# A fused attention and mixture-of-experts layer: expert stages ahead of the attention heads, and half of the combination beside the heads

## The chip, the cores and the metric

The kernel runs on one core of a Trainium2 chip. The metric is the device time of one execution in microseconds. The engines are TensorE (PE, with its weight loads PEld), VectorE (DVE), ScalarE (ACT), GpSimd (POOL) and SyncE (SP, which here only issues DMAs). Each engine works through its own instruction list in order, and waits on semaphores for the others.

## What is computed

Input x is 8 batches of 512 tokens of 256 numbers, that is 32 token tiles of 128 tokens. All is float32. In short:

```python
xn = layernorm(x)
# attention: 16 heads, low-rank queries (128) and keys/values (64), rotary part of 64, causal softmax
attn_out = attention(xn) @ W_o
# experts: 32 experts of width 96, 6 chosen for each token, and a shared one of width 192
scores = sigmoid(xn @ gate_w); w, i = top_k(scores, 6); w = w / sum(w)
routed = sum over the 6 chosen e of w[e] * (silu(xn @ wg[e]) * (xn @ wu[e])) @ wd[e]
shared = (silu(xn @ sg) * (xn @ su)) @ sd
out = x + attn_out + routed + shared
```

## The kernel before

A float32 product is made of three matmuls of rounded parts (`product3`, lines 58 to 63: high by high, low by high, high by low), so each operand is split into a high and a low part by ACT and DVE. The kernel is a row of blocks; a block begins when every engine has ended the one before.

1. Weights, then `project` (line 228): for each of 8 batches the layer norm, the latents and the routing. SP stores the results to memory and fills the first half of `sorted_x` with zeros, 2 MB for each batch (line 335). At its end DVE works out which expert owns which tile and in which row of `sorted_x` each token goes (`routes`, from line 588). I call this stage tokens.
2. `heads` (line 641): 8 batches, 16 heads each. A step of the pipeline is one head, two steps are a pair. `pipeline` runs the first 8 steps alone, then a loop from the middle of one batch to the middle of the next. PE's step is scores, queries or their transposes, scores, values, scores, transposes of the probabilities, scores; DVE takes the maxima (line 1066), turns queries by rope (lines 1047 to 1052), copies and divides. Beside this POOL scatters all 32 token tiles into `sorted_x`, 6 indirect DMAs each (line 816), and SP fills the second half of `sorted_x` with zeros in the first batches (line 773). The residual sum goes to `res_dram`.
3. `weights_and_shared` (line 1381): 16 steps. Each loads and splits the weights of two experts and computes the shared expert of one token tile.
4. `sorted_tiles` (line 1502): 256 tiles of 128 rows sorted by expert, in two groups of 128, each group from 16 token tiles. While the second group is computed, `Combine` adds up the six expert rows of 15 token tiles of the first group: POOL gathers them (line 1333), DVE finds the six shares (line 1353) and adds (line 1374).
5. `shared_and_rest` (line 1738): the shared expert of the last 16 token tiles, and the combination of the last 17.

The lines that set a token tile's combination are:

```python
for k in ks:
    ins = dve.scalar_tensor_tensor(self.found[:, k, :], self.slot_of[:, m, :], self.slot_top[:, m, k:k + 1],
                                   self.comb[:, m, :], ALU.is_equal, ALU.mult, accum_out=self.share[:, k:k + 1])
...
dve.wait_ge(self.s["summed"], TOPK * m + TOPK + k)
dve.scalar_tensor_tensor(self.sum[par][:], self.rows[par][u][:, place, :], self.share[:, k:k + 1],
                         last[:], ALU.mult, ALU.add).then_inc(self.s["summed"], 1)
```

## Time and profile before

| | us |
|---|---|
| median of 3 runs (1851.81 to 1855.62) | 1854.5 |
| the profiled execution, its own time | 1855.27 |
| its span, first to last instruction | 1853.5 |
| PE busy | 1467.5 (79%) |
| DVE busy | 1115.1 (60%) |
| ACT busy | 930.9 (50%) |
| POOL busy | 569.7 (31%) |

The granted clock of PE over the whole is 0.895 of full speed. The shares of the whole span hide what differs from stage to stage, so the work below is read stage by stage: which engine is busy there, at which clock, and how busy the DMA engines are.

### The profile page before, as it was taken

The page shows a single profiled execution, that of the slowest core. Times are in us where ns is not written, and L with a number is a line of the kernel's source. Part 1 is how long each engine was busy: PE and PEld are TensorE (multiplying, and loading weights), DVE is VectorE, ACT ScalarE, POOL GpSimd, SP SyncE. Part 2 cuts the span into 40 slices and gives each one's busy share as a digit, 9 for nine tenths or more (in the row PEclk, how much of TensorE's full clock was granted, in tenths as well). Part 3 has the DMA queues.
Part 4 walks back from the last instruction along what each step waited for, and adds up shares of the span by engine and source line. Part 5 has one row for each costly group of instructions (what it writes and reads, how often), then busy time and mean ns, then how long its engine had stood idle before and what let it go on. Part 6 is the DMA issues. An engine that isn't in the chain of part 4 may idle for free. (4 is left out here: it accounts for less than half of the span.)

```text
span 1853.5 us, 37109 instructions
## 1 busy us (share of the span) xinstructions
PE 1467.5 (79%) x10112; PEld 1248.0 (67%) x10113; DVE 1115.1 (60%) x4335; ACT 930.9 (50%) x2739; POOL 569.7 (31%) x640
## 2 busy tenths in 40 slices
PE   2663499989899999999999986799998888885340
PEld 2552378868688777878878764588887777774330
DVE  2896276656566676766666644555555666664464
ACT  1330276656566666666666644366665555552000
POOL 1120043433343343433433430000001433335565
PEclk8676699999999999999999997799999998998665
DMA  3993611321411111111111107654545665665553
GB/s 143 329 375 123 232 56 56 113 88 47 147 58 60 49 52 60 58 62 58 58 54 47 50 21 239 201 163 157 159 153 163 197 184 183 193 194 179 148 168 112
DMA packets 169539, 240.29 MB, mean 130 GB/s; under 512 B 16786, under 2 KB 142738, under 8 KB 165010
## 3 DMA queue, kind: packets, MB, share of 16 engines
q1 hardware_dynamic: 146322, 183.61, 29.9%
q0 software_dynamic: 18432, 50.36, 8.8%
q10 hardware_dynamic: 4608, 4.20, 0.8%
q8 instruction: 82, 1.34, 0.3%
q14 instruction: 95, 0.78, 0.1%
HBM read 115.42 MB, written 122.68 MB: 128 GB/s over the span
## 5 line engine op out<-in xcount | busy, mean ns | idle before, releaser
L988 ACT ACTIVATE prob<-prob,negmax 128x512 f32<-128x512 f32 (+3 forms) x512 | 285.3, 559 | 302.1 <-DVE negmax L1066 300.8
L1066 DVE CUSTOM_DVE_ANT_0 prob<-ps,mask_add 128x512 f32<-128x512 f32 (+3 forms) x512 | 244.2, 485 | 147.4 <-issue 144.2
L61 PE MATMUL ps<-kt_hi,qt_hi 128*128 (+4 forms) x512 | 188.5, 368 | 21.7 <-issue 18.7
L816 POOL DMA_INDIRECT sorted_x<-xn_row,row_no x192 | 188.3, 981 | 49.4 <-issue 45.0
L826 POOL TENSOR_TENSOR spread<-rinv,one 128x512 f32<-128x512 f32 x64 | 66.6, 1040 | 380.0 <-DVE rinv L1072 380.0
L63 PE MATMUL ps<-kt_hi,qt_lo 128*128 (+4 forms) x512 | 166.4, 325 | 0.0
L62 PE MATMUL ps<-kt_lo,qt_hi 128*128 (+4 forms) x512 | 166.0, 324 | 0.0
L910 PE MATMUL ps<-ident,prob 128*128 128x128 f32 x1280 | 160.6, 273 | 0.0
L926 PE MATMUL ps<-pt,nkv 128*64 128x512 f32 (+3 forms) x1024 | 152.0, 439 | 2.3 <-DVE lat L1084 2.3
L910 PEld LDWEIGHTS ps<-ident,prob 128*128 128x128 f32 x1280 | 143.5, 140 | 0.2 <-ACT prob L988 0.2
L1001 ACT ACTIVATE pt<-ps 128x1024 f32<-128x1024 f32 (+2 forms) x130 | 130.4, 1003 | 19.8 <-PE ps L910 16.9
L1680 ACT ACTIVATE hidden<-ps 128x96 f32<-128x96 f32 x256 | 64.5, 252 | 124.7 <-PE ps L63 108.3
L926 PEld LDWEIGHTS ps<-pt,nkv 128*64 128x64 f32 x1024 | 68.2, 136 | 86.5 <-issue 74.6
L1692 ACT ACTIVATE rows_out<-ps 128x256 f32<-128x256 f32 x256 | 98.5, 385 | 49.7 <-PE ps L63 34.7
L1076 DVE COPY pt<-ps 128x512 f32<-128x512 f32 x128 | 88.0, 687 | 57.1 <-PE ps L910 57.1
L61 PEld LDWEIGHTS ps<-kt_hi,qt_hi 128*128 128x128 f32 x512 | 98.2, 192 | 35.1 <-issue 30.2
L821 POOL TENSOR_TENSOR lat_lo<-lat,lat_hi 128x512 fp32r<-128x512 f32 x64 | 81.7, 1277 | 109.6 <-ACT lat_hi L1006 109.6
L1720 DVE TENSOR_TENSOR act_f<-hidden,ps 128x96 f32<-128x96 f32 x256 | 64.8, 253 | 80.8 <-ACT hidden L1680 61.9
L1331 POOL TENSOR_TENSOR carrier_b<-one_b 128x1 f32 x30 | 5.9, 196 | 343.9 <-DMA sorted_y<-rows_out 223.4
L61 PE MATMUL ps<-wq_hi,nqt 128*128 128x256 f32 x256 | 74.5, 291 | 45.2 <-DMA nqt<-nqt_dram 45.2
L1635 PE MATMUL ps<-ident,rows_in 128*128 128x128 f32 x512 | 103.6, 285 | 6.2 <-DMA rows_in<-sorted_x 5.9
L1333 POOL DMA_INDIRECT rows_c<-sorted_y,idx_c x102 | 99.6, 976 | 27.5 <-issue 26.5
(240 smaller groups left out, 4481.4 us busy)
## 6 DMA issues: line engine op xcount, KB each, us to landing
sorted_x<-zeros SPq DMA_DIRECT2D x16, 2048.0 KB, 9.4
rows_in<-sorted_x SPq DMA_DIRECT2D x128, 256.0 KB, 2.8
sorted_y<-rows_out SPq DMA_DIRECT2D x128, 256.0 KB
nqt<-nqt_dram SPq DMA_DIRECT2D x16, 512.0 KB
raw_gu<-in_wgu SPq DMA_DIRECT2D x16, 384.0 KB, 4.0
x_in<-in_x SPq DMA_DIRECT2D x8, 512.0 KB, 4.2
xn_dram<-xn SPq DMA_DIRECT2D x8, 512.0 KB, 5.0
xnt_dram<-xnt_hi SPq DMA_DIRECT2D x16, 256.0 KB, 4.7
```

Source lines behind the costliest of these rows:

```text
L61: pe.matmul(out, lh, rh, start=first, stop=False, **kw)
L62: pe.matmul(out, lh, rl, start=False, stop=False, **kw)
L63: return pe.matmul(out, ll, rh, start=False, stop=last, **kw)
L816: pool.indirect_dma_start(sorted_x, bass.IndirectOffsetOnAxis(ap=row_no[par][:, k:k + 1], axis=0), xn_row[par][:], None).then_inc(scattere ...
L910: mm = pe.transpose(pt_ps[:, at:at + P], prob[:, g % 2, qt, kt * P:(kt + 1) * P], ident[:])
L926: mm = pe.matmul(o_ps[par * KVR:(par + 1) * KVR, kt * P:S], nkv[half][:, kt, :], pt[:, par, PT_AT[kt]:PT_AT[kt] + w], start=kt == 0, stop= ...
L988: act.activation(prob[:, i, qt, 0:w], prob[:, i, qt, 0:w], ACT.Exp, bias=negmax[:, i, qt:qt + 1], scale=-1.0, accum_out=rowsum[:, g // 2 % ...
L1001: act.activation(pt[:, g % 2, lo:hi], pt_ps[:, lo:hi], ACT.Copy).then_inc(pt_act, 1)
L1066: dve.tensor_tensor_reduce(prob[:, i, qt, 0:w], s_ps[k % 2][:, 0:w], mask[:, S - w:S], -1.0, -MASKED, ALU.add, ALU.min, negmax[:, i, qt:qt ...
L1333: pool.indirect_dma_start(self.rows[par][u][:, k, :], None, self.sorted_y, bass.IndirectOffsetOnAxis(ap=self.idx[par][u][:, k:k + 1], axis ...
L1635: mm = pe.transpose(xt_ps[par][:, kc * P:(kc + 1) * P], rows_in[j // 2 % AHEAD][:, par, kc * P:(kc + 1) * P], ident[:])
L1692: act.activation(rows_out[d % 2][:, (j - 3) % 2, :], y_ps[1 - par], ACT.Copy)\
```

## The change

The stages change places. After tokens comes `weights_and_shared`, now with all 32 token tiles and the weights of one expert a step, while POOL scatters the 16 token tiles of the first group. Then `sorted_tiles`: beside its first half POOL writes zeros where rows are unused (16 indirect DMAs in place of the plain fill of the second half) and scatters the second group; beside its second half the 15 token tiles are combined as before, into `base_dram`. `heads` comes last, adds its residual to `base_dram` and writes `out`; beside its first batches 17 token tiles are gathered and added. `shared_and_rest` is gone. As the heads now run later, keys, query weights and output weights are stored to memory in tokens and loaded again. Cut to its core:

```diff
@@ build
-            attention(nc, ctx, sem, x, wc, ...)
-        experts(nc, sem, wgu, wd, ...)
+            tokens(nc, ctx, sem, x, wc, ...)
+        experts(nc, sem, x, wgu, wd, ...)
+        with ExitStack() as ctx:
+            heads(nc, ctx, sem, rope, nqt_dram, kt_dram, nkv_dram, wq_dram, wvo_dram, base_dram, sorted_y, ...)
@@ project, SP
                 sp.dma_start(nqt_dram[i], nqt[:].bitcast(F32)).then_inc(nq_stored, 16)
+                sp.dma_start(kt_dram[i], kt[:].bitcast(F32)).then_inc(kt_stored, 16)
             load(0)
+            for k in range(2):
+                sp.dma_start(wq_dram[k], wq_s[k][:].bitcast(F32)).then_inc(kept, 16)
+                sp.dma_start(wvo_dram[k], wvo_s[k][:].bitcast(F32)).then_inc(kept, 16)
@@ routes: nine DVE instructions for the rows to be filled with zeros, behind the tiles' owners
+                chain(dve.tensor_copy(pad_no[:], pad_f[:]))
@@ heads, the token tile of a step: four steps (phases) for one token tile
+        def token_tile(self, g):
+            if not self.gathers or g >= NH:
+                return None
+            if g < NH // 2 and self.last is None:
+                return (0, 0, 0, g) if g < QUART else None
+            i, at = (self.now, g - NH // 2) if g >= NH // 2 else (self.last, g + NH // 2)
+            j, phase = divmod(at, QUART)
+            return QUART * i + (j + 1), (j + 1) % 2, 2 * i + (j + 1) // 2, phase
@@ heads, pipeline
+            batches(0, QUART, True)
+            if after_gathers is not None:
+                after_gathers()
+            batches(QUART, B - 1, False)
@@ heads, SP
-            def fill(i):
-                sp.dma_start(zero_part[i], zeros[:]...)
+                sp.wait_ge(s_ready, TT * NH * b + TT * NH // 2)
+                sp.dma_start(kt[0][:].bitcast(F32), kt_dram[b + 1]).then_inc(kt_loaded[0], 16)
@@ heads, POOL, in a step after the spreading and the low parts
-                if g < NH and par == 1:
-                    scatter(bt.now, g // 4, g // 2 % 2)
+                if bt.token_tile(g):
+                    c, buf, _, phase = bt.token_tile(g)
+                    if phase == 0:
+                        gather(c, buf)
@@ heads, DVE, in a step after the residual and ahead of the maxima
-                    dve.tensor_copy(row_no[q % 2][:], slot_no[:, TT * bt.now + q, :]).then_inc(row_no_ready, 1)
+                    if phase == 0:
+                        copy_indices(c, buf, n)
+                    if phase < 2:
+                        find_shares(c, buf, HALFK * phase)
+                    else:
+                        for k in range(HALFK * (phase - 2), HALFK * (phase - 1)):
+                            add_row(c, buf, n, k)
@@ weights_and_shared
-    EC = NE // GT
+    EC = NE // NT
+            def load_row(t):
+                if t >= 2:
+                    sp.wait_ge(scattered[t % 2], 16 * TOPK * (t // 2))
+                sp.dma_start(xn_row[t % 2][:], xn_dram[t]).then_inc(row_loaded[t % 2], 16)
+        @block.gpsimd
+        def _(pool):
+            for t in range(GT):
+                pool.wait_ge(row_loaded[t % 2], 16 * (t // 2) + 16)
+                for k in range(TOPK):
+                    pool.indirect_dma_start(sorted_x, bass.IndirectOffsetOnAxis(ap=slot_no[:, t, k:k + 1], axis=0),
+                                            xn_row[t % 2][:], None).then_inc(scattered[t % 2], 16)
@@ sorted_tiles, SP (load_row as above, once in 4 pairs) and POOL
+                    if ms[-1] is None and d % EVERY == 0:
+                        load_row(i, d // EVERY)
+            for k in range(2 * PADS):
+                pool.indirect_dma_start(chunks, bass.IndirectOffsetOnAxis(ap=pad_no[:, k:k + 1], axis=0),
+                                        zeros[:], None).then_inc(padded, 16)
@@ the last stage
-def shared_and_rest(nc, ctx, shared, combine):
-    ...
```

## Rows read from the trace of the kernel before

**Rows 1.** Busy time by stage; columns: stretch, engines busy (x), PEclk, DMA share, GB/s

```profile
0.00:202.60 202.60, 89.00 (x448) 74.26 (x449) 119.06 (x512) 43.61 (x172) 25.04 (x29) 0.71 0.61 222
202.60:1117.30 914.70, 839.81 (x6144) 703.11 (x6144) 584.99 (x2241) 560.38 (x1410) 341.60 (x353) 0.98 0.21 73
1117.30:1194.60 77.30, 55.44 (x224) 41.09 (x224) 42.78 (x100) 33.27 (x83) 0.00 (x0) 0.76 0.79 240
1194.60:1418.00 223.40, 208.45 (x1577) 187.73 (x1577) 118.82 (x401) 144.86 (x524) 0.10 (x1) 0.96 0.50 158
1418.00:1679.40 261.40, 215.58 (x1496) 191.88 (x1496) 159.85 (x674) 135.63 (x500) 94.33 (x120) 0.92 0.60 184
1679.40:1853.50 174.10, 59.24 (x224) 49.93 (x224) 89.58 (x408) 13.15 (x50) 108.61 (x137) 0.62 0.52 155
```

**Rows 2.** POOL's end of the heads block (L763) and of the last (L1767)

```profile
L763 POOLq DRAIN  x1: 8034/8034/8034, 1102.4 to 1102.4; - x1
L1767 POOLq DRAIN  x1: 18298/18298/18298, 1835.0 to 1835.0; - x1
```

**Rows 3.** Tokens: one batch's busy time, and SP's wait at the stage's end

```profile
112.20:125.10 12.90, 8.94 (x40) 7.71 (x40) 11.87 (x57) 4.22 (x21) 2.65 (x2) 0.66 1.05 376
SPq L313 <- DMA tile_expert<-owner: 36.1, 1, 36.1
```

**Rows 4.** Weights and shared: four steps' busy time; what ACT waits for, 1130 to 1190

```profile
1145.00:1160.00 15.00, 12.26 (x48) 9.31 (x48) 9.44 (x22) 7.45 (x20) 0.00 (x0) 0.77 0.91 279
ACT wgu_hi L1475 <- DMA raw_d<-in_wd: 29.7, 14, 3.0
```

**Rows 5.** Indirect DMAs on POOL: two lines (duration ns min/median/max), one in the timeline

```profile
L1333 POOL DMA_INDIRECT rows_c<-sorted_y,idx_c x102: 940/949/1263, 1680.5 to 1843.8; - x102
L816 POOL DMA_INDIRECT sorted_x<-xn_row,row_no x192: 957/963/1501, 223.9 to 1087.9; - x192
1703.36 0.94 POOL L1333 DMA_INDIRECT rows_c<-sorted_y,idx_c  x1 [0.31 <-issue]
```

**Rows 6.** Sorted tiles: PE's transposes in 1215:1400 and 1440:1670, and POOL's DMA queue in 1440:1670

```profile
L1635 PE MATMUL ps<-ident,rows_in 128*128 128x128 f32 x222 | 43.2, 276 | 0.0
L1635 PE MATMUL ps<-ident,rows_in 128*128 128x128 f32 x223 | 46.0, 289 | 0.0
q0 software_dynamic: 4032, 11.02, 17.2%
```

**Rows 7.** Last stage, DVE's groups of the combination

```profile
L1374 DVE SCALAR_TENSOR_TENSOR sum_c<-rows_c,share_c,sum_c 128x256 f32<-128x256 f32 x85 | 41.6, 489 | 8.2 <-DMA rows_c<-sorted_y,idx_c 5.6 <-DVE sum_c L1374 0.5
L1353 DVE SCALAR_TENSOR_TENSOR found_c<-slot_of,slot_top,comb 128x32 f32 (+1 forms) x102 | 18.9, 244 | 0.1
```

**Rows 8.** Heads, one pair of steps in the timeline: DVE twice, then PE

```profile
702.20 0.55 DVE L1066 CUSTOM_DVE_ANT_0 prob<-ps,mask_add 128x384 f32<-128x384 f32 x1 [1.25 <-issue]
705.96 0.69 DVE L1084 TENSOR_TENSOR lat<-ps,pt 128x512 f32<-128x512 f32 x1
706.89 2.37 PE L926 MATMUL ps<-pt,nkv 128*64 128x512 f32 x16
```

**Rows 9.** Heads: a pair without residual; and the last gather's issue with its first reader

```profile
661.44 1.04 POOL L826 TENSOR_TENSOR spread<-rinv,one 128x512 f32<-128x512 f32 x1 [4.17 <-DVE rinv L1072]
670.25 0.29 DVE L1066 CUSTOM_DVE_ANT_0 prob<-ps,mask_add 128x128 f32<-128x128 f32 x1
...
1843.83 1.08 POOL L1333 DMA_INDIRECT rows_c<-sorted_y,idx_c  x1 [0.30 <-issue]
1846.70 1.52 DVE L1374 SCALAR_TENSOR_TENSOR sum_c<-rows_c,share_c,sum_c 128x256 f32<-128x256 f32 x3 [2.10 <-DMA rows_c<-sorted_y,idx_c]
```

**Rows 10.** Heads: PE's idle time at three loop starts, in the timeline

```profile
377.64 0.79 PE L61 MATMUL ps<-kt_hi,qt_hi 128*128 x1 [6.32 <-issue]
493.29 0.79 PE L61 MATMUL ps<-kt_hi,qt_hi 128*128 x1 [6.28 <-issue]
824.08 0.49 PE L61 MATMUL ps<-kt_hi,qt_hi 128*128 x1 [2.17 <-issue]
```

More of the change, by code:

```diff
@@ L1181, with __init__ @@
+            sorted_tiles(nc, part, sem, combine, wgu_s, wd_s, sorted_x, sorted_y, tile_expert, xn_dram,
+                         slot_no, pad_no, ident, ps)
 class Shared:
-    def __init__(self, nc, ctx, tag, times, sems, sgu, sd, xnt_dram, res_dram, base_dram, ident, ps):
+    def __init__(self, nc, ctx, sem, sgu, sd, x, xnt_dram, base_dram, ident, ps):
         def two(name, shape, dt=F32):
-            return [ctx.enter_context(nc.sbuf_tensor(f"{name}{i}_{tag}", shape, dt)) for i in range(2)]
+            return [ctx.enter_context(nc.sbuf_tensor(f"{name}{i}", shape, dt)) for i in range(2)]
@@ L1398, in steps @@
             step(n, n % 2, n // 2)
-        with eng.Fori(2, GT // 2) as i:
+        with eng.Fori(2, NT // 2) as i:
             for par in range(2):
                 step(2 * i + par, par, i)
-        for n in range(GT, GT + 2):
+        for n in range(NT, NT + 2):
             step(n, n % 2, n // 2)
     def tile(n, lag):
-        return not isinstance(n, int) or 0 <= n - lag < GT
+        return not isinstance(n, int) or 0 <= n - lag < NT
     def parts(n, par, half):
@@ L1579, in body @@
                     r = PAIRS * i + d
+                    if ms[-1] is None and d % EVERY == 0:
+                        load_row(i, d // EVERY)
+                    if ms[-1] is None and not isinstance(i, int) and d == PAIRS - AHEAD + 1:
+                        for par in range(2):
+                            sp.wait_ge(scattered[par], 16 * TOPK * ((ROWS // 2 + 1) * i - 1))
                     if not (isinstance(i, int) and r + AHEAD - 1 >= NTILE // 2):
```

506 lines of the change are left out of this document (269 added, 237 removed).

## Prediction, made before the result was known

> **What bounds the kernel now.** I read busy time by stage first [rows 1]. The six stages take 202.6, 914.7, 77.3, 223.4 and 261.4 (the two halves of the sorted tiles) and 174.1 us, together 1853.5. PE fills 92% of heads and 93% of the first half of the sorted tiles, at a clock of 0.98 and 0.96: there PE sets the pace. The last stage is different: PE is busy for 59.2 of 174.1 us at a clock of 0.62, DVE for 89.6, POOL for 108.6. It waits for POOL's gathers, and no other work lies beside them. The change takes this stage away and lays its work beside others. So the question is what its two parts, 16 shared tiles and 17 combined tiles, cost in their new places, and what the reordering adds in memory traffic.
>
> **The last stage goes: minus 174.1 us.** All of it lies on the path, as blocks follow one another. Its end includes POOL's drain, which ran until 1853.3, some 5 us past the last sum [rows 2]. The new end is the end of heads, where POOL's drain (8.0 us from 1102.4) was over before PE's last matmuls, so only the store of the residual and the block's end follow, and these are inside the 914.7 already.
>
> **Tokens: plus 12 us.** Added are eight stores of keys (0.5 MB each), 4 MB of weights at the start, and nine small DVE instructions. The nine (2 to 3 us) lie behind the owners' step; SP waits 36.1 us for the two tiny `tile_expert` stores issued before them [rows 3], and DVE was idle in that wait, so they cost nothing, and 3 us if that wait were gone. A batch takes 12.9 us, with DVE busy 11.87 and the DMA engines' share at 1.05, 376 GB/s [rows 3]: both are full. 0.5 MB more at 376 GB/s is 1.4 us a batch, 11 us for eight, if DMA binds; if the queue had room it would be some 0.5 us, 4 us in all. The 4 MB at the start would take 11 us at that rate, but fall where the first batch has hardly any traffic; 1 to 11 us. I take 9 + 3 = 12, ends 3 and 22.
>
> **Weights and shared: plus 70 us.** There are 32 steps in place of 16. Four steps took 15 us, 3.75 each, at a DMA share of 0.91 and 279 GB/s, and ACT waited 29.7 us for weights [rows 4]. A step moved 1.09 MB: weights 0.58, tokens 0.25, residual and sum 0.25. A new step moves half the weights (0.29), the same 0.5, and of the scatter 0.38 and its rows 0.06: 1.23 MB. At 279 GB/s and full use (279/0.91 = 307) that is 4.0 us. POOL needs six indirect DMAs for two steps, each 0.95 with a gap of 0.31 [rows 5]: 7.6 us, 3.8 a step, so it is nearly as late. PE's 12.26 us for four steps [rows 4] are 3.1 a step and don't bind. I take 4.05 us a step: 130, and the 77.3 - 60 = 17 us of filling and emptying stay, 147 in all. The SP queue now has a wait for the scatter of two tiles ago ahead of each row load, with the loads of tokens and weights queued behind it; it is satisfied while POOL keeps to 7.6 us. Ends: 3.75 (plus 60 us) and 4.8 a step (plus 93).
>
> **Sorted tiles: plus 10 us.** The second half keeps its work. Beside the first half POOL now issues 112 indirect DMAs: 112 x 1.26 = 141 us, inside 223.4. They carry 21 MB, at the q0 price of 17.2% of 230 us for 11.02 MB [rows 6], 3.6 us a MB, 76 us of the DMA engines: the share goes from 0.50 to some 0.85. No engine of that half waited for loads, so this hides. What doesn't is SP: the third row load waits until POOL has done 16 zero DMAs and the first token tile (22 x 1.26 = 28 us, and landing), and SP's loads and stores for PE and ACT stand behind it; again at the end, when SP waits for the last scatter. Each block is 8 to 11 us with some 5 to 9 us of loads ahead: 5 us each. Ends 0 and 35 (if the larger share slows each tile as the second half's traffic may have).
>
> **Heads: plus 34 us.** Three terms. (a) The zero fills go. PE stood for 6.3 us at the first two loop starts, while 4 MB of fill were under way, and 2.2 at a later one [rows 10]: minus 2 x 4.2 = 8.5. (b) At the start PE waits for half a MB of query weights more: plus 1; the rest (keys, 3.5 MB) lands while the first steps run. (c) DVE gets, in four steps for each of 17 token tiles: phase 0 a copy (as before) and three shares, 3 x 0.244 = 0.7 us; phase 1 0.7; phases 2 and 3 three additions, 3 x 0.489 = 1.5 each [rows 7]. They stand ahead of the maxima and, in odd steps, of the division `lat`. In an even step DVE had 1.25 us idle behind the first maxima [rows 8]: phase 0 hides, phase 2 shows 0.25. In an odd step DVE ends `lat` at 706.65 and PE begins its values, which need that bank, at 706.89: slack 0.24, so phase 1 shows 0.46 and phase 3 1.26. Sum 1.95, times 17 is 33 us. PE has no other slack to give it back. Then the gathers. POOL's six follow the spreading, at 662.5 [rows 9]: some 0.2 for the carrier, 6 x 1.26 to issue; the last begins at 669.0, and a reader can start 2.87 us after its issue begins (1843.83 to 1846.70) [rows 9]: 671.9. DVE comes for them at 670.5 in pairs without a residual, so it waits 1.4 us, of which some 1 shows, for 8 of 17 tiles: 8 us. In pairs with one it comes 2 us later and doesn't wait. Heads: -8.5 + 1 + 33 + 8 = 34. Ends: nothing of (c) shows (minus 8), and all of it does, 17 x 4.4 + 16 = 91 (plus 83). For comparison, the same additions beside the sorted tiles: 223 transposes, 112 tiles, in 230 us against 112 in 185 [rows 6] is 45 us for 14 token tiles, 3.2 us each of some 4.7; heads' 1.95 is less because I can name the idle time.
>
> **The sum.** 1853.5 - 174.1 + 12 + 70 + 10 + 34 = 1805.4 us of span. The profiled execution took 1855.27 for a span of 1853.5, 1.8 more, so 1807.2 against 1855.27, and the median shown is 0.8 below that: 1806 us, 2.6% faster.
>
> **The rivals.** *A, as above*: 0.61. *B, PE hides DVE's new work*: DVE goes from 64% of heads to some 80% in the first batches, still short of full; then (c) is nothing: 1806 - 42 = 1764 us. Against it speaks the slack of 0.24 us; 0.14. *C, memory traffic binds the early stages*: the shared steps take 4.8 us (+23), the sorted tiles lose 25 more, tokens 10 more: 1806 + 48 or less, say 1840. For it speaks a share of 0.91 before anything is added, against it the half-size weights; 0.15. *D, the gathered rows come late*: DVE waits for them with the maxima, and so PE, queued behind it. 42 us of lead plus what I count already make this decide from 48/17 = 2.8 us of further lateness per token tile. A gather that took 1.9 us on POOL instead of 0.95 would be 5.7 us later, 17 x 5.7 = 97: 1903 us. Against it: a scatter beside the heads took 0.963 us, a gather in the last stage 0.949 [rows 5], so the busy DVE does not slow POOL; 0.10.
>
> The Trainium skill has a rule that speaks for D and against this change. "SBUF — State Buffer", sections "SBUF: two separate sides" and "Who interferes with whom", says in substance that POOL can't write the descriptors of its DMAs while DVE runs an instruction that takes the ports both share, and gives 620 ns against 3100 ns for such a DMA. By that factor of five, six gathers would be late by far more than D's 2.8 us and the kernel slower than before. The trace doesn't show it: 963 against 949 ns.
>
> **How the numbers follow.** The likeliest is A, 1806. B reaches down to 1764, C up to 1840, my bounds of the single terms some 15 to 20 us each way for those that go together. I leave out the ends of B and C and all of D: 1758 to 1848, and the range reaches lower than higher about 1806 because B is a whole case and its lower bounds (tokens 9 less, weights 10 less) go with it. A difference of 0.2%, 3.7 us, is about what a measurement of this kernel can tell from none. Faster: A and B, and most of C: 0.87. Same: 0.02. Slower: D and the tail of C: 0.11.
>
> **What would show it.** Tokens end near 215 us. The weights stage takes 147 with a DMA share of 0.9 or more, and POOL nearly without gaps. The first half of the sorted tiles has two gaps of some 5 us on PE, at its start and end, and no others. In heads the first four loop batches take some 8 us longer each than the last three, PE waits before its values (L926 of before) for DVE's division, and the 6.3 us stalls are 2.2. It would be wrong if PE's waits in heads were behind gathered rows (D), if all batches took the same time (B), or if PE in the sorted tiles waited for loads (C).

## The result, and the profile after

The changed kernel took 1944.8 us (median of 4 runs, 1943.2 to 1953.0) beside 1853.2 for the kernel before (median of 4, 1850.8 to 1855.6): a ratio of 1.050, 95% interval 1.047 to 1.054. It is 5% slower, where I forecast 2.6% faster. Its profiled execution took 1943.6 us for a span of 1941.8.

The same kind of table as [rows 1], for the kernel after: a stretch, then its length, the busy time of PE, PEld, DVE, ACT and POOL with the number of instructions, the granted clock of PE, the share of the DMA engines and GB/s. The five stretches are tokens, weights and shared tiles, the two halves of the sorted tiles, and heads.

```profile
0.00:211.80 211.80, 87.36 (x448) 73.07 (x449) 123.82 (x527) 42.74 (x172) 25.42 (x30) 0.71 0.68 252
211.80:388.50 176.70, 112.94 (x448) 90.02 (x448) 64.86 (x196) 48.87 (x163) 93.84 (x96) 0.67 0.71 235
388.50:721.60 333.10, 252.33 (x1579) 229.19 (x1580) 119.96 (x401) 149.20 (x525) 108.61 (x114) 0.79 0.54 175
721.60:980.40 258.80, 217.77 (x1496) 195.08 (x1494) 158.75 (x673) 136.44 (x500) 92.63 (x120) 0.90 0.61 186
980.40:1941.80 961.40, 848.27 (x6144) 708.32 (x6144) 647.59 (x2534) 562.96 (x1411) 249.51 (x250) 0.98 0.17 53
```

Against [rows 1], stage by stage, with what I had forecast in brackets: tokens +9.2 (+12), weights and shared +99.4 (+70), first half of the sorted tiles +109.7 (+10), second half -2.6 (0), heads +46.7 (+34), last stage -174.1 (-174.1). The sum is +88.3, against -48. Of the 136 us between them, 100 lie in one term, the first half of the sorted tiles, and 29 in the shared stage. Neither stage ran out of anything that I had counted: the DMA share is 0.54 and 0.71, not 0.85 and 0.9, and POOL's scatters keep their pace (961 ns, as in [rows 5]), while POOL itself mostly waits for the next token tile's rows, which SP loads once in four pairs of sorted tiles:

```profile
L1780 POOL DMA_INDIRECT sorted_x<-xn_row_e,slot_no x96 | 92.3, 961 | 201.1 <-DMA xn_row_e<-xn_dram 169.3
```

**One burst of scatters.** Eight sorted tiles took 19.2 us, against 13.2 in the kernel before ([rows 6]: 112 tiles in 185 us). In the 7.6 us in which POOL issues the six scatters of a token tile PE does 36 matmuls and transposes; in the 11.6 us behind it, 66, at a clock of 0.75:

```profile
483.40:491.00 7.60, 4.72 (x36) 3.97 (x35) 1.83 (x7) 2.37 (x8) 5.76 (x6) 0.94 0.60 183
491.00:502.60 11.60, 10.35 (x66) 9.52 (x66) 5.38 (x19) 6.52 (x24) 0.00 (x0) 0.75 0.47 143
```

From the timeline of that burst (lines between these are left out): start, duration, engine, line, operation, names, and in brackets the idle time before it and what ended it.

```profile
488.05 0.28 PE L67 MATMUL ps<-wgu_hi,xt_e0lo 128*128 x1
488.49 0.96 POOL L1780 DMA_INDIRECT sorted_x<-xn_row_e,slot_no  x1 [0.30 <-issue]
489.17 0.25 ACT L1863 ACTIVATE hidden<-ps 128x96 f32<-128x96 f32 x1 [2.55 <-PE ps L67]
489.45 0.26 DVE L1903 TENSOR_TENSOR act_f<-hidden,ps 128x96 f32<-128x96 f32 x1 [2.37 <-ACT hidden L1863]
489.76 0.31 PE L1836 MATMUL ps<-ident,act_f 128*96 128x128 f32 x1 [1.44 <-issue]
```

The reader is to see the first and third lines. The last matmul of the gate and up product ends at 488.33, ACT has long been idle, and yet it begins the activation that waits for that product at 489.17, 0.84 us later. No load is waited for. A sorted tile passes through ten handings-over between PE, ACT and DVE, and four of them go out from PE. In these rows only that kind is late: DVE begins 0.03 us after ACT has ended (489.42 to 489.45), PE 0.05 us after DVE (489.71 to 489.76). In the whole half, wherever DVE stood waiting for ACT's part of a tile, it began within 0.04 us of ACT's end, while ACT came up to 1.4 us late behind PE's transposes. PE's ends are modelled in this profile, so these rows don't tell whether PE's signal is late or its result.

**Heads.** The engine waits of PE in heads (engine, line, what it waited for: us in total, times, longest) are mostly where I had put them: the values (L1020, L926 of before) wait for DVE's division, the waits that end in "issue", those at loop starts among them, are at most 2.2 us in place of the 6.3 of [rows 10], and the first wait is for query weights. The longest in total (L961) is no news, the kernel before has it too (33.0 us). But the scores wait 22.2 us for DVE's maxima (`negmax`), 2.3 in the kernel before, and there I had allowed 0.25 us a token tile.

```profile
PE ps L961 <- DVE qp L1157: 35.0, 62, 3.0
PE ps L1020 <- DVE lat L1220: 25.7, 27, 2.0
PE ps L65 <- DVE negmax L1202: 22.2, 22, 2.2
PE ps L65 <- DMA wq_lo_h<-wq_dram: 12.1, 1, 12.1
PE ps L65 <- issue: 7.3, 10, 2.2
```

The stores of the residual, one a batch, show the two kinds of batches: 124.3 and 123.6 us apart with gathered tiles beside them, 110.4 without. I had said some 8 us between them; it is 14.

```profile
1153.16 0.41 SPq L880 DMA_DIRECT2D out<-res  x1
1277.45 0.41 SPq L880 DMA_DIRECT2D out<-res  x1
...
1633.84 0.41 SPq L880 DMA_DIRECT2D out<-res  x1
1744.28 0.41 SPq L880 DMA_DIRECT2D out<-res  x1
```

### The profile page after: what moved, and what is told of

Same layout as the page of the kernel before. It is cut to its first block and busy times, and to the rows that moved or that the text cites. A ratio compares the mean times of both kernels' runs of the same rounds, so it can differ in the third digit from the quotient of the medians.

```text
span 1941.8 us, 37055 instructions
## 1 busy us (share of the span) xinstructions
PE 1518.7 (78%) x10112; PEld 1295.7 (67%) x10113; DVE 1115.0 (57%) x4331; ACT 940.2 (48%) x2770; POOL 570.0 (29%) x610
## 3 DMA queue, kind: packets, MB, share of 16 engines
q0 software_dynamic: 20736, 58.75, 9.4%
## 5 line engine op out<-in xcount | busy, mean ns | idle before, releaser
L1202 DVE CUSTOM_DVE_ANT_0 prob<-ps,mask_add 128x512 f32<-128x512 f32 (+3 forms) x512 | 244.1, 487 | 150.2 <-issue 145.8
L65 PE MATMUL ps<-kt,qt_hi 128*128 128x512 f32 (+3 forms) x512 | 190.7, 372 | 29.1 <-DVE negmax L1202 22.2
L1020 PE MATMUL ps<-pt,nkv 128*64 128x512 f32 (+3 forms) x1024 | 152.0, 438 | 28.2 <-DVE lat L1220 25.7
L66 PE MATMUL ps<-kt,qt_hi 128*128 128x512 f32 (+3 forms) x512 | 166.2, 325 | 0.0
L67 PE MATMUL ps<-kt,qt_lo 128*128 128x512 f32 (+3 forms) x512 | 165.6, 323 | 0.0
L1780 POOL DMA_INDIRECT sorted_x<-xn_row_e,slot_no x96 | 92.3, 961 | 201.1 <-DMA xn_row_e<-xn_dram 169.3
L1020 PEld LDWEIGHTS ps<-pt,nkv 128*64 128x64 f32 x1024 | 74.7, 136 | 108.0 <-issue 89.8
L1004 PEld LDWEIGHTS ps<-ident,prob 128*128 128x128 f32 x1280 | 144.5, 141 | 0.2 <-ACT prob L1093 0.2
L1106 ACT ACTIVATE pt<-ps 128x1024 f32<-128x1024 f32 (+2 forms) x130 | 130.2, 1002 | 16.1 <-PE ps L1004 13.2
L1594 POOL DMA_INDIRECT sorted_x<-xn_row,slot_no x96 | 93.8, 978 | 127.3 <-DMA xn_row<-xn_dram 99.2
L65 PEld LDWEIGHTS ps<-kt,qt_hi 128*128 128x128 f32 x512 | 97.7, 191 | 49.0 <-DVE negmax L1202 29.3
L65 PE MATMUL ps<-wgu_hi,xt_e1hi 128*128 x256 | 89.6, 350 | 48.5 <-DVE xt_e1lo L1897 36.1
L1818 PE MATMUL ps<-ident,rows_in 128*128 128x128 f32 x512 | 113.0, 307 | 7.3 <-DMA rows_in<-sorted_x 5.8
L1836 PE MATMUL ps<-ident,act_f 128*96 128x128 f32 x256 | 80.5, 314 | 47.1 <-issue 26.4
```

The source lines that it names most:

```text
L65: pe.matmul(out, lh, rh, start=first, stop=False, **kw)
L66: pe.matmul(out, lh, rl, start=False, stop=False, **kw)
L67: return pe.matmul(out, ll, rh, start=False, stop=last, **kw)
L1004: mm = pe.transpose(pt_ps[:, at:at + P], prob[:, g % 2, qt, kt * P:(kt + 1) * P], ident[:])
L1020: mm = pe.matmul(o_ps[par * KVR:(par + 1) * KVR, kt * P:S], nkv[half][:, kt, :], pt[:, par, PT_AT[kt]:PT_AT[kt] + w], start=kt == 0, stop= ...
L1106: act.activation(pt[:, g % 2, lo:hi], pt_ps[:, lo:hi], ACT.Copy).then_inc(pt_act, 1)
```

## The experiments

The theories at the start: **H**, while POOL issues indirect DMAs and they are under way, every handing-over between the other engines takes longer, whatever the bytes (the rows above show it too wide: only those out of PE); **B**, the added bytes; **S**, the row loads and waits on SP's queue. As blocks follow one another, a stage can be read alone, and one kernel can carry a different alteration in each. Runs were spread over several chips, and that turned out to matter as much as any alteration, so I give for each run the time of the kernel before beside it.

**Without indirect DMAs.** The six scatters or gathers of a token tile are gone, and the pads; a small POOL instruction raises the semaphore.

```diff
-                for k in range(TOPK):
-                    pool.indirect_dma_start(sorted_x, bass.IndirectOffsetOnAxis(ap=slot_no[:, GT + t, k:k + 1], axis=0),
-                                            xn_row[t % 2][:], None).then_inc(scattered[t % 2], 16)
+                pool.memset(idle_second[:, t:t + 1], 0.0).then_inc(scattered[t % 2], 16 * TOPK)
```

> The changed kernel without any indirect DMA: the scatters of both groups, the pads, and the gathers of the second half of the sorted tiles and of heads are left out, and the semaphores are raised by small POOL instructions instead. Left out of the computation: what these rows would carry (DVE adds rows of zeros, with the same instructions). The row loads on SP's queue stay, with their waits. The second half of sorted_x is filled with zeros at the end of the tokens stage (16 MB), which makes that stage some 30 to 50 us longer, so only the stages behind it are read. Theory H (while POOL issues indirect DMAs and they are under way, every handing over between PE, ACT and DVE takes about 1 us longer, whatever the bytes; PE's clock falls after the stalls): the first half of the sorted tiles falls from 333 to 223-230 us with a clock of 0.95, the shared stage from 177 to 125-135 us. Theory B (the added bytes): the same here. Theory S (the waits and row loads on SP's queue): both stay near 333 and 177. Second half of the sorted tiles (259): 223-230 if the gathers cost its 35 us over the first half of before, 255-260 if DVE's additions do, as I wrote. Heads (961): 950 if gathers only cost the 8 us of lateness of my forecast; 915-930 if H holds there too.

Measured, beside 1786.3 of the kernel before: shared 114.2, first half 224.8, second half 210.7, heads 941.1. On this chip S falls: the row loads and their waits are all there. The second half was a surprise: some 50 us less than in either kernel's own profile (258.8 and 261.4), with all of DVE's additions in it.

**Narrow rows.**

```diff
+NARROW = 16
...
-                    pool.indirect_dma_start(sorted_x, bass.IndirectOffsetOnAxis(ap=slot_no[:, GT + t, k:k + 1], axis=0),
-                                            xn_row[t % 2][:], None).then_inc(scattered[t % 2], 16)
+                    pool.indirect_dma_start(narrow, bass.IndirectOffsetOnAxis(ap=slot_no[:, GT + t, k:k + 1], axis=0),
+                                            xn_row[t % 2][:, 0:NARROW], None).then_inc(scattered[t % 2], 16)
```

> The changed kernel with every indirect DMA kept, same count, same indices, but 64 bytes of a row instead of 1024 (scatters into and gathers from a tensor of its own; the pads stay as they are). Left out of the computation: the other 960 bytes of each row (the additions run over zeros there). Sorted_x is filled with zeros at the end of tokens, as in the kernel without indirect DMAs. H: what counts is that POOL issues them, so the first half of the sorted tiles stays at 320-335 us and the shared stage at 170-177. B: the bytes are a sixteenth, so the first half falls to 225-235 and the shared stage to 130. The second half and heads go the same way: unchanged (259, 961) by H, as without indirect DMAs by B.

**Direct DMAs on POOL's queue.**

```diff
-                    pool.indirect_dma_start(sorted_x, bass.IndirectOffsetOnAxis(ap=slot_no[:, GT + t, k:k + 1], axis=0),
-                                            xn_row[t % 2][:], None).then_inc(scattered[t % 2], 16)
+                    pool.dma_start(sorted_x[(GSORT + TOPK * t + k) * P:(GSORT + TOPK * t + k + 1) * P],
+                                   xn_row[t % 2][:]).then_inc(scattered[t % 2], 16)
```

> The changed kernel with every scatter and gather turned into a direct DMA of the same bytes on POOL's queue (fixed rows; the pads stay indirect). Left out: the rows go to and come from wrong places. H in its narrow form (only indirect DMAs, whose descriptors POOL writes itself, do it): first half of the sorted tiles 225-240 us, shared 125-140. B: same bytes, so 320-335 and 170-177. If direct DMAs on POOL's queue are written by POOL as well and cost about as much per DMA as the indirect ones, H too gives 320-335, and the narrow kernel decides alone.

**Additions over one column.**

```diff
-                dve.scalar_tensor_tensor(total[par][:], rows[par][:, k, :], share[par][:, k:k + 1],
-                                         (base if k == 0 else total)[par][:], ALU.mult, ALU.add)
+                dve.scalar_tensor_tensor(total[par][:, 0:1], rows[par][:, k, 0:1], share[par][:, k:k + 1],
+                                         (base if k == 0 else total)[par][:, 0:1], ALU.mult, ALU.add)
```

> The changed kernel with all DMAs, but the six additions of a token tile run over 1 column instead of 256, in the second half of the sorted tiles and in heads (left out of the computation: the other 255 columns of the combination). The first half and the shared stage stay at 333 and 177 by every theory. My forecast took the second half's 35 us over the first half of before as the additions' price: then it falls from 259 to 223-230. If the gathers cost it (H), it stays at 250-259. Heads: my forecast has 1.95 us of additions and shares visible per token tile, most of it additions: 961 falls to 930-935; if H rules there, it stays at 950-961.

The four ran one after the other on one chip. Shared, first half, second half, heads: narrow 141.0, 239.0, 210.4, 948.5; direct 131.2, 239.5, 210.9, 943.9; additions over one column 143.5, 243.5, 211.6, 931.3. The last kernel's first two stages are the changed kernel's, word for word, and took 143.5 and 243.5, not 176.7 and 333.1. Nothing that I had altered could do that.

```profile
215.10:358.60 143.50, 92.09 (x448) 77.94 (x448) 64.00 (x196) 48.04 (x163) 95.85 (x96) 0.82 0.87 290
358.60:602.10 243.50, 215.36 (x1579) 195.58 (x1580) 119.35 (x401) 144.58 (x525) 108.44 (x115) 0.92 0.73 240
```

**Both kernels again.** So I ran the two kernels unaltered, and the changed one with one part undone: no scatters of the second group (the first diff above) and no pads.

```diff
-            for k in range(2 * PADS):
-                pool.indirect_dma_start(chunks, bass.IndirectOffsetOnAxis(ap=pad_no[:, k:k + 1], axis=0),
-                                        zeros[:], None).then_inc(padded, 16)
+            pool.memset(idle_pads[:], 0.0).then_inc(padded, 32 * PADS)
```

> The changed kernel unaltered, in the company of the kernel before, because the stages that four altered kernels share with it word for word ran shorter there than in its own profile (the shared stage 143.5 us where only the sums were cut, against 176.7), and the kernel before took 1786 us beside them, not 1853. Theory P (the length of the early stages depends on something outside the kernel, the chip or where its tensors lie): 1770 to 1800 us, ratio 0.99 to 1.01, with a shared stage of 144 and a first half of the sorted tiles of 220-240. Theory F (the ratio of 1.05 belongs to the kernel): 1875 where before takes 1786, with the first half at 333 us again.

> The kernel before unaltered, for a profile under the same conditions as the altered kernels. If it takes 1786 us again: P says that the 67 us under 1853 lie in the stages with POOL's indirect DMAs beside short handings-over, the second half of the sorted tiles (261 down to 225-235) and the last stage (174 down to 140-150), while tokens, heads and the first half, which has no indirect DMA, keep 203, 915 and 223. If the difference lay in PE's clock or in heads, heads would be 50 us shorter.

> The changed kernel without the second group's scatters and pads (left out: these rows; the second half of sorted_x is filled with zeros at the end of the tokens stage, which makes that stage 30 to 50 us longer). Only the first half of the sorted tiles has something taken away. H (handings-over are slower while indirect DMAs run): that half goes to 223-230, wherever it stands with them; the shared stage is as in the changed kernel beside it (177 or 144), the second half 259 or what it is there.

On this chip the changed kernel is the faster one, by 0.6%: 1771.6 us (4 runs, 1769.0 to 1772.3) against 1781.6 (7 runs, 1779.1 to 1785.1), ratio 0.994, 95% interval 0.992 to 0.996. Theory P holds, F falls. The stages of the kernel before there, in the order of [rows 1]:

```profile
0.00:205.90 205.90, 86.25 (x448) 72.48 (x449) 119.12 (x512) 43.55 (x172) 25.01 (x29) 0.72 0.60 218
205.90:1119.90 914.00, 838.51 (x6144) 701.21 (x6144) 585.07 (x2241) 560.51 (x1410) 341.50 (x353) 0.98 0.21 73
1119.90:1196.50 76.60, 52.93 (x224) 38.62 (x224) 42.80 (x100) 33.27 (x83) 0.00 (x0) 0.81 0.78 242
1196.50:1419.20 222.70, 208.12 (x1577) 187.63 (x1577) 118.85 (x401) 144.99 (x524) 0.10 (x1) 0.96 0.50 158
1419.20:1633.30 214.10, 197.15 (x1497) 175.88 (x1496) 161.87 (x674) 136.67 (x500) 92.20 (x120) 0.98 0.74 225
1633.30:1782.80 149.50, 58.00 (x224) 49.37 (x224) 88.74 (x408) 13.01 (x50) 108.48 (x137) 0.63 0.60 180
```

Against [rows 1] two stages differ by more than 4 us: the second half (214.1 for 261.4) and the last stage (149.5 for 174.1). They are the two in which POOL's indirect DMAs run beside short handings-over; heads, with 192 scatters, doesn't differ (914.0 for 914.7). And the changed kernel's stages there:

```profile
0.00:215.60 215.60, 87.74 (x448) 72.91 (x449) 123.82 (x527) 42.60 (x172) 25.42 (x30) 0.69 0.67 247
215.60:360.10 144.50, 92.54 (x448) 78.82 (x448) 64.58 (x196) 48.45 (x163) 95.83 (x96) 0.82 0.88 288
360.10:603.60 243.50, 214.62 (x1579) 194.57 (x1580) 119.62 (x401) 144.97 (x525) 108.69 (x114) 0.92 0.74 240
603.60:817.90 214.30, 195.91 (x1496) 174.73 (x1494) 161.04 (x673) 135.57 (x500) 92.33 (x120) 0.99 0.73 224
817.90:1770.50 952.60, 844.72 (x6144) 706.70 (x6144) 650.13 (x2534) 563.29 (x1411) 250.14 (x250) 0.98 0.17 53
```

A burst of six scatters and the time up to the next one, in the same kernel on this chip: PE does 59 matmuls in the 7.6 us, not 36, its clock stays at 1.00, and the eight tiles take 13.4 us, not 19.2. The activation that waited 0.84 us above follows its product (ends 457.89) within 0.04 us.

```profile
429.10:436.70 7.60, 7.25 (x59) 6.70 (x59) 3.80 (x13) 5.03 (x18) 5.78 (x6) 1.00 0.74 228
436.70:442.50 5.80, 5.58 (x45) 4.96 (x45) 3.57 (x12) 3.79 (x16) 0.00 (x0) 1.00 0.65 204
```

```profile
457.62 0.27 PE L67 MATMUL ps<-wgu_hi,xt_e1lo 128*128 x1
457.93 0.25 ACT L1863 ACTIVATE hidden<-ps 128x96 f32<-128x96 f32 x1 [0.40 <-PE ps L67]
```

With the second group's scatters and pads undone the first half took 224.2, the other stages 143.4, 214.2 and 953.4, as they were.

The end of the shared stage there (in the changed kernel on this chip; duration in ns min/median/max, then first and last start) shows what sets its length. The last matmul begins at 347.99, but POOL issues its last scatter at 349.4, its drain at the block's end then takes 7.9 us, and only behind that does the next stage begin, at 360.1:

```profile
L1594 POOL DMA_INDIRECT sorted_x<-xn_row,slot_no x96: 958/963/1341, 223.1 to 349.4; - x96
L1552 POOLq DRAIN  x1: 7902/7902/7902, 352.0 to 352.0; - x1
```

Here POOL itself is the last to end: 96 scatters at 1.26 us are 121 of the 144.5 us, and 8 more are the drain. On the slow chip PE's work and POOL's drain end within 1.5 us of each other.

From here on I speak of two kinds of chips. On **kind 1** the kernel before takes 1777 to 1786 us (three chips), on **kind 2** 1851 to 1864 (four chips more, and the runs of the case itself). None lay between. Each chip was met in one session only, so "kind of chip" is a name: a difference of session or of where the tensors lie would look the same. What makes the kind no run shows.

**The causes on kind 2.** Which kind a run meets can't be chosen, so the next kernels ask one question a stage, with the edits shown above in other combinations.

> The changed kernel with a different alteration in each stage, as blocks follow one another and each stage is read alone. Shared stage: no scatters. First half of the sorted tiles: no pads, the 96 scatters kept but with 64 bytes a row instead of 1024 (into a tensor of its own). Second half: no gathers, additions kept. Heads: no gathers, additions kept. All these rows are left out of the computation; sorted_x and the narrow tensor are filled with zeros at the end of tokens, which lengthens that stage by 30 to 50 us. Two answers by the time of the kernel before beside it. Where that is 1780 to 1786: shared 114, first half 235-240 (count, not bytes, costs 10-15 us), second half 211, heads 940. Where it is 1850 to 1855, H (on such a chip each handing-over takes longer while indirect DMAs are under way, whatever the bytes): shared 114-120, first half 300-333 with 64 bytes as with 1024, second half down from 259 to 211-220, heads down from 961 to 940-950. If bytes are the cause there: first half 225-240, the second half down as well. If such a chip is slow by itself, without any indirect DMA: shared stays above 140 and the second half at 259.

It met kind 2 (1858.2 beside it):

```profile
245.80:359.60 113.80, 84.85 (x448) 71.99 (x448) 63.53 (x196) 47.57 (x163) 1.57 (x16) 0.89 0.84 255
359.60:683.90 324.30, 247.17 (x1589) 225.21 (x1590) 120.15 (x403) 148.33 (x527) 94.72 (x102) 0.82 0.39 118
683.90:890.50 206.60, 192.66 (x1486) 171.71 (x1484) 162.05 (x672) 136.66 (x497) 5.70 (x30) 1.00 0.56 175
890.50:1833.30 942.80, 843.63 (x6144) 705.61 (x6144) 649.49 (x2534) 563.21 (x1411) 154.41 (x150) 0.99 0.12 40
```

Without scatters the shared stage is as on kind 1 (113.8 and 114.2), so the chip is not slow by itself, and S falls here too, as the row loads and their waits are in it. With 64 bytes a row, and no pads, the first half still takes 324.3, at a DMA share of 0.39: bytes are not the cause, B falls. Without gathers, with all additions, the second half drops from 258.8 to 206.6.

> The changed kernel, altered by stages. Shared stage: the 96 scatters kept, with 64 bytes a row. First half of the sorted tiles: no pads; the scatters turned into direct DMAs of the same bytes on POOL's queue (fixed rows). Second half: gathers with 64 bytes a row, additions kept. Heads: gathers kept, additions over one column in place of 256. Rows and sums left out accordingly; the zero fill at the end of tokens as in mix_a. Where the kernel before takes 1780-1786 beside it: 141, 235-240, 211 and 931 us. Where it takes 1850-1858, H (each DMA that POOL issues while others pass work to and fro costs about 1 us, bytes don't count) has shared 165-177, the second half 250-259 with 64 bytes as with 1024. For the first half it leaves two answers that this run tells apart: 300-325 if every DMA written by POOL does it, 225-250 if only indirect ones do. Heads there: 961 less the additions' visible part, 930 by my forecast's sizes.

> The changed kernel, altered by stages. Shared stage as it is. First half of the sorted tiles: the six scatters of a token tile no longer in one burst of 7.6 us but one for every 1.33 tiles that PE turns (for the first twelve token tiles). Second half: gathers kept, additions over one column (left out: the rest of these sums). Heads: the six gathers of a token tile in two threes, one step apart, as the kernel before scattered its rows. Where the kernel before takes 1780-1786: 144, 235-243, 212 and 945-953 us. Where it takes 1850-1858: if the loss is a price of each DMA (H), the first half stays at 315-335 however they lie; if it comes from bursts, in which descriptors pile up, it falls to 240-280. Second half: 250-259, since additions cost nothing there (mix_a lost 52 us of 259 by leaving out the gathers alone). Heads: 961 by a price of each DMA, 945 by bursts.

Both met kind 1 (1777.1 beside them). The direct and narrow forms: shared 140.6 (narrow), first half 236.4 (direct, no pads), second half 206.4 (narrow), heads with additions over one column 927.5. The other kernel's edit is a wait ahead of each scatter and, in heads, two threes in place of six gathers:

```diff
+                    if t < 12:
+                        pool.wait_ge(xt_ready, 8 * t + 2 + 4 * k // 3)
...
-                    if phase == 0:
-                        gather(c, buf)
+                    if phase < 2:
+                        gather(c, buf, phase)
```

It gave 143.4, 244.1 (spreading does nothing on kind 1), 211.7, and heads of 995.9, 43 us more than with six gathers in one go, where I had expected none: the last three rows now come a step later, and DVE waits for them ahead of its maxima. Of DVE's waits in the first batches of heads (813.9 to 1400 us), those for gathered rows; the changed kernel on kind 1 has 3.7 us in 4 such waits, none longer than 1.2:

```profile
DVE total L1187 <- DMA rows<-sorted_y,idx: 31.3, 12, 4.5
```

This is the mechanism of rival D.

> The changed kernel, altered by stages. Shared stage: direct DMAs on POOL's queue in place of the scatters, same bytes, fixed rows. First half of the sorted tiles: pads and scatters kept, each scatter gated on the tiles PE has turned, so that they lie 1.33 tiles apart. Second half: direct DMAs in place of the gathers, additions kept. Heads: gathers kept, additions over one column. Rows and sums are wrong or left out accordingly. Where the kernel before takes 1780-1786: 131, 244, 211 and 928-931 us, as in the altered kernels before. Where it takes 1850-1858, against 177, 333, 259 and 961 of the changed kernel: if every DMA that POOL writes does it, shared 155-177 and the second half 245-259; if only indirect ones do, 115-135 and 206-220. First half 315-335 if each scatter has its price, 240-290 if the bursts do it. Heads 930-940.

It met kind 2 (1857.5 beside it):

```profile
216.00:347.90 131.90, 91.61 (x448) 78.01 (x448) 64.48 (x196) 48.22 (x163) 51.59 (x96) 0.82 0.94 315
347.90:637.30 289.40, 234.27 (x1579) 209.83 (x1580) 118.75 (x401) 143.59 (x525) 108.81 (x114) 0.86 0.62 202
637.30:850.00 212.70, 196.47 (x1496) 175.80 (x1494) 161.46 (x673) 136.69 (x500) 54.78 (x120) 0.98 0.72 226
850.00:1793.50 943.50, 845.71 (x6144) 710.65 (x6144) 620.91 (x2535) 562.11 (x1411) 249.84 (x250) 0.98 0.17 54
```

DMAs of the same bytes from the same queue, only not indirect, cost far less: 131.9 for 176.7 in the shared stage (at a DMA share of 0.94), and 212.7 for 258.8 in the second half. In the second half that is all but 6 us of the 52; in the shared stage 18 us above the 113.8 without scatters stay, and no run says whether by bytes, by count or by POOL's drain, which is still 7.9 us. The number of packets on POOL's queue is the same in both forms (20736). For the first half the direct form was not run on kind 2. There, with the scatters of twelve of the sixteen token tiles spread out in place of bursts, it takes 289.4, not 333.1. So part of the price belongs to bursts, and a fixed price for each DMA is too simple.

**Indices in order.** What was left: is it the indirect form, or that the 128 rows of one DMA lie apart?

```diff
+            pool.iota(row_of[:], pattern=[[P, TOPK * GT]], base=GSORT * P, channel_multiplier=1).then_inc(row_of_ready, 1)
...
-                    pool.indirect_dma_start(sorted_x, bass.IndirectOffsetOnAxis(ap=slot_no[:, GT + t, k:k + 1], axis=0),
+                    pool.indirect_dma_start(sorted_x, bass.IndirectOffsetOnAxis(ap=row_of[:, TOPK * t + k:TOPK * t + k + 1], axis=0),
```

> The changed kernel with the scatters of both groups kept as indirect DMAs, same count and bytes, but with indices in order: each DMA writes 128 rows that lie one behind the other, where the real one writes 128 rows apart from each other (left out: the rows' true places). Pads, gathers and sums are as in the changed kernel. Theory I (the indirect form itself): shared and the first half stay as in the changed kernel, 144 and 243 where the kernel before takes 1780-1786, 177 and 333 where it takes 1850-1858. Theory A (rows that lie apart): they go to the times with direct DMAs, 131 and 236, or 132 and 223-240. The second half and heads are unaltered, 214 and 953, or 259 and 961.

Kind 2 (1856.8 beside it), 1942.3 us in all, with the shared stage and first half where they were:

```profile
208.40:386.90 178.50, 115.62 (x448) 93.70 (x448) 65.25 (x196) 48.82 (x163) 94.23 (x97) 0.65 0.72 233
386.90:719.50 332.60, 248.96 (x1579) 226.19 (x1580) 120.28 (x401) 148.40 (x525) 108.97 (x115) 0.80 0.55 176
```

Theory I holds for both: it is not where the rows lie. With the two runs before it that leaves the indirect form itself, shown for the shared stage and the second half by the direct DMAs, and for the first half by ruling out bytes and addresses. As this kernel does the changed kernel's work in the changed kernel's order, but for the places of the scattered rows, it also shows the loss a second time, on a further chip (1942.3 against 1856.8).

**A version with the scatters elsewhere.** Heads in two parts: batches 5 to 7 behind tokens, with the pads and 24 token tiles' scatters beside them; batches 0 to 4 at the end, with the gathers. The core of it:

```diff
+            heads(nc, ctx, early_sem, "_1", LATER, B - LATER, False, rope, nqt_dram, kt_dram, nkv_dram, wq_dram, wvo_dram,
...
         experts(nc, sem, x, wgu, wd, sgu, sd, sorted_x, sorted_y, tile_expert, xn_dram, xnt_dram, base_dram, res_dram,
...
+            heads(nc, ctx, sem, "_2", 0, LATER, True, rope, nqt_dram, kt_dram, nkv_dram, wq_dram, wvo_dram,
...
+                if not with_gathers and g < NH:
+                    scatter(bt.now, g, g % 2)
```

> A version meant to keep the change's gain and take the scatters away from where they hurt. Heads in two parts: batches 5 to 7 run right behind tokens, and beside them POOL writes the pads and scatters 24 of the 32 token tiles, three rows of DMAs a step as in the kernel before; then weights and shared tiles (with the other 8 tiles' scatters), the sorted tiles (no scatters), and heads of batches 0 to 4 with the 17 gathered tiles. Nothing is left out. By the prices measured so far, where the kernel before takes 1780-1786: from the changed kernel's 1771 off 19 us in the first half and 15 in shared, on 22 for starting heads twice and some 10 for scatters beside heads: 1769 (1755-1785), ratio 0.985-1.0. Where the kernel before takes 1850-1858: from 1944 off 110 and 32, on 22 and 144 x 0.18 = 26: 1850 (1820-1870). If the first half stays above 235 us without scatters beside it, the prices are wrong.

> The kernel with heads in two parts once more, for the other kind of chip, if this is one. Where the kernel before takes 1850-1858 it took 1872. Where it takes 1780-1786 I expect, by the prices there (19 us of the first half and 15 of the shared stage saved against the changed kernel, 22 us for starting heads twice, and scatters at six a pair beside heads, which cost 39 us in three batches on the other kind of chip, a third of that here): 1771 - 34 + 22 + 13 = 1772 (1760-1785), no better than the changed kernel.

> The kernel with heads in two parts, a third time, since both chips so far were of the kind on which the kernel before takes 1855 (there 1872 and 1855, where the changed kernel takes 1942 to 1945). If this chip is of the other kind: 1772 (1760-1785) against 1771 to 1772 of the changed kernel and 1780-1786 of the kernel before. If not: 1850-1875 again.

All three met kind 2, on three chips: 1872.4 beside 1857.5 (ratio 1.008, interval 1.005 to 1.010), 1854.9 beside 1856.8 (0.998, 0.997 to 1.000), 1854.3 beside 1858.3 (0.998, 0.996 to 1.000). That is 4 to 5% under the changed kernel's 1944.8, and at best 0.2% under the kernel before; the first lies just outside what I expected (1820 to 1870), the others inside. In the first of them the first half of the sorted tiles is back at 223.2, so the prices of that stage were right. The first part of heads with its shared stage took 519.7 us there and 504.7 on the other two chips; its three batches alone took 394.1 and 384.7, where three eighths of 914.7 and the 22 us for starting twice are 365. The scatters beside them are twice as dense as in the kernel before, which may be the reason; no run tested it. What it does on kind 1 wasn't measured. A version that beats both kernels on both kinds I didn't find.

## Why the forecast was wrong, step by step

The price of the indirect DMAs, as the stage with them less the stage without, over their number. (For the first half on kind 2 the stage without is that of the kernel before, which has no row loads either; on kind 1 these cost at most 2 us, 224.2 and 224.8 against 222.7.)

| stage | DMAs | kind 2 | kind 1 |
|---|---|---|---|
| shared | 96 | (176.7 - 113.8) / 96 = 0.66 us | (144.5 - 114.2) / 96 = 0.32 |
| first half, with pads | 112 | (333.1 - 223.4) / 112 = 0.98 | (243.5 - 224.2) / 112 = 0.17 |
| second half | 90 | (258.8 - 206.6) / 90 = 0.58 | (214.3 - 210.7) / 90 = 0.04 |
| heads | 102 | (961.4 - 942.8) / 102 = 0.18 | (952.6 - 941.1) / 102 = 0.11 |

In the shared stage on kind 1 the 0.32 is no price for others: there POOL's own row of scatters and its drain set the stage's end.

**Sorted tiles, +10 against +109.7: the step that failed.** I wrote that the added transfers hide because no engine of that half waited for loads. That was true and beside the point: nobody waits for the transfers, but while POOL issues them ACT gets PE's results late, and with ACT the chain behind it. The term put the effect of 112 indirect DMAs on PE, ACT and DVE at nothing, without a row for it. My ends of 0 and 35 came from two stops of SP and from bandwidth; the mechanism at work was not among them, nor among the rivals. C, the nearest, priced bandwidth, and at a share of 0.54 there was none short. (Its three terms, 23, 25 and 10, also come to 58 and not to the 48 that stands there.) Of the 5.8 us that eight tiles lose (19.2 against 13.4), PE's missing work in the burst is 7.25 - 4.72 = 2.5; the 66 matmuls behind it, at the other chip's pace of 5.58 / 45, would take 8.2 and not 10.35, so the clock of 0.75 costs 2.2; the rest is further stalls. That division is an estimate from these rows. The low clock follows the stalls: in five bursts in a row, from 446 to 541 us, it is 0.91 to 1.00 while POOL issues and 0.70 to 0.75 behind it.

**The evidence that I read wrongly** was in the profile of before. Its second half takes 45 us more than its first for 14 tiles, and I put that down to DVE's additions (3.2 us a token tile of some 4.7). On kind 2, leaving out the gathers alone takes 52 us off that half, with every addition in place; on kind 1, additions over one column take off 2.7 (214.3 to 211.6). The 45 us were the price of 84 gathers, 0.54 us each. With that reading, 112 scatters and pads beside the first half come to 60 us in place of my 10, and the forecast to 1856, no faster than before, ahead of anything for the 96 of the shared stage.

**Shared, +70 against +99.4.** The sum was right on kind 1 (+67.9, 3.98 us a step, DMA share 0.88) and its reason was not: I had bandwidth bind, but a sixteenth of the scatters' bytes gives 141.0 for 144.5, and none of them 114.2. Count, not bytes, is 27 of the 30 us. What binds there is the term that I had called "nearly as late", POOL's 3.8 us a step, with a drain behind it that I hadn't counted; that the sum came out right was partly luck. On kind 2 the late handings-over come on top. A step without scatters takes some 3.0 us, so the 3.75 of the kernel before, with its larger weights, was no floor for it.

**Heads, +34 against +46.7.** The places were right, the sizes roughly. DVE's additions: of my 33 us for additions and shares, the additions are 26 (phases 2 and 3), and measured 17.9 on kind 2, and 21.3 and 25.1 in two runs on kind 1. So B, that nothing of them shows, is out, and the slack of 0.24 us was the right row to look at. Gathers: 8 forecast, 18.6 and 11.5 measured. The stalls by the fills go as said. The start doesn't quite: PE's first matmul comes 8.3 us into heads (988.73 - 980.4) in place of 5.2 (207.76 - 202.6), so 3 us and not 1. Of the 46.7 us, 18.6 are gathers and 17.9 additions; the other 10 (the start, the fills that are gone, the shares, and what an addition over one column still costs) I didn't take apart.

**Tokens, +12 against +9.2**, and **the last stage, -174.1**, as forecast. But the last stage is worth only 149.5 on kind 1, and there my terms for what is added, 12 + 70 + 10 + 34 = 126, stand against a measured 137. Even there the gain would have been forecast too high (48 us for the 12 by which the two spans differ), mostly because the stage that goes costs 25 us less there.

**Rival D** compared 963 with 949 ns and found that DVE doesn't slow POOL. It doesn't in any run: 961 ns beside the sorted tiles, and no indirect DMA of any run took more than the 1501 ns of [rows 5]. The rule of the Trainium skill, "SBUF — State Buffer", section "SBUF: two separate sides", with its 3100 ns, showed nowhere; the page limits it to DVE instructions that take the shared ports as well, and which of this kernel's do, no run sorts out. I never asked the question the other way round, whether POOL holds up the rest.

## What to carry to other kernels

When two stretches with the same work differ and several things were added to the longer one, don't price one of them by the whole difference: here DVE's additions took the blame for POOL's gathers, and the next term was built on it. An indirect DMA has a price for the engines beside it that neither its duration nor its bytes show; put such DMAs beside work like these heads (0.1 to 0.2 us each, and 192 scatters beside them cost no more on one kind of chip than on the other) and not beside a short chain PE, ACT, DVE (up to 1 us each). That heads are spared because PE has other work queued while ACT waits for its result is my reading, not a run's. And measure a few per cent on more than one chip: the same two kernels gave 1.050 and 0.994.

## What the runs showed of the hardware

- Chips (or sessions on them) differ: the kernel before takes 1777 to 1786 us on three and 1851 to 1864 on the others, the changed one 1771.6 and 1944.8. Apart from 3 to 4 us in tokens the whole difference lies in stages with indirect DMAs; of these, heads of the kernel before agrees all the same (914.0 and 914.7), and so does the first half of its sorted tiles, which has none (222.7 and 223.4).
- On the second kind an indirect DMA beside short handings-over costs the stage up to 0.98 us, with 64 bytes a row nearly as with 1024 (324.3 us, without pads, and 333.1), and with rows in order as with rows apart (332.6). A direct DMA of the same bytes on the same queue costs far less (second half: 212.7 against 206.6 without any; shared stage: 131.9 against 113.8), and POOL is busy with it for 0.54 us (51.59 / 96) against 0.98 (93.84 / 96).
- POOL's drain at the end of the shared stage takes 7.9 us behind 96 scatters, direct ones too, and 0.05 us where there are none.
- A handing-over from PE to ACT that takes 0.04 us on one chip took 0.84 on the other in the middle of a burst of scatters, while those from ACT to DVE stayed at 0.03. By what way (the semaphores, POOL's reading of indices, the writing of descriptors) wasn't tried and stays open.
